# Attention: one turned unit in eight copied by ScalarE, six probability slots, and layer three's denominators inverted once a head

## The reference

```python
attn = jnp.einsum('bhqd,bhkd->bhqk', q, k)          # q, k, v quantised to 255 levels
attn = jax.nn.softmax(attn.astype(jnp.float32), axis=-1)
attn = _fq_unsigned(attn, axis=-1)                  # rounded to 0..255 of the row's maximum
out = jnp.einsum('bhqk,bhkd->bhqd', attn, v)
```

```python
kv_summary = jnp.einsum('bhsd,bhse->bhde', k, v)
k_sum = k.sum(axis=-2)
z = 1.0 / (jnp.einsum('bhld,bhd->bhl', q, k_sum)[..., None] + EPS)
attn = jnp.einsum('bhld,bhde->bhle', q, kv_summary) * z
out = attn * gate @ Wo.T
```

## Time and profile before

| what | value |
|---|---|
| median of 3 runs | 1017.53 us (1016.32 to 1019.76) |
| the profiled execution, its own time | 1022.85 us |
| its span | 1020.3 us |
| busy: TensorE, VectorE, ScalarE, GpSimd | 865.2, 736.0, 446.2, 166.8 us |
| layer two's attention loop, first row maximum to the end of the last | 579.35 to 762.64 us |
| layer three's attention | 842.82 to 898.56 us |

### The profile page before, as it was taken

One profiled execution on the slowest core, in us unless ns is written; L12 is line 12 of the kernel. 1 busy time (PEld: TensorE's weight loads), 2 busy tenths in 40 slices (PEclk: granted clock), 3 DMA queues, 4 the chain that ended last, 5 costly groups with the idle time before them and its releaser, 6 DMA issues.

```text
span 1020.3 us, 11627 instructions
## 1 busy us (share of the span) xinstructions
PE 865.2 (85%) x4214; PEld 512.5 (50%) x4214; DVE 736.0 (72%) x974; ACT 446.2 (44%) x679; POOL 166.8 (16%) x251
## 2 busy tenths in 40 slices
PE   5989894489889999989899677788888988779898
PEld 3434662244655555545455344344444657654566
DVE  1776558964557787787678898899994546658777
ACT  2214446642324422221223588789883434622111
POOL 1000000000013532425200162111111000001412
PEclk9899885589979999999899855555558999969999
DMA  8502003100132222240112989987771000000000
GB/s 266 197 3 44 1 0 50 19 2 7 19 48 43 36 35 25 54 59 10 22 25 42 170 150 176 155 146 146 139 145 30 9 1 0 1 1 1 10 11 21
DMA packets 211612, 59.13 MB, mean 58 GB/s; under 512 B 192398, under 2 KB 209892, under 8 KB 211556
## 3 DMA queue, kind: packets, MB, share of 16 engines
q1 hardware_dynamic: 211444, 58.23, 29.5%
q10 hardware_dynamic: 112, 0.17, 0.1%
HBM read 20.62 MB, written 1.05 MB: 21 GB/s over the span
## 4 chain that ended last, share of the span: by engine, by line
PE 52%; DVE 25%; ACT 10%; issue 7%; DMA 4%; POOL 1%; ACTq 1%; DVEq 0%; SPq 0%; POOLq 0%
PE ps L946 48%; ACT xc L1889 5%; DMA arena<-xc 4%; DVE arena L2593 3%; DVE arena L2227 1%; PE ps L1077 1%; DVE arena L2602 1%; PE ps L1389 1%; DVE xc L2399 1%; ACT arena_split L1806 1%; DVE sq L2506 1%; DVE sq L2503 1%; PE ps L472 1%; DVE xn_t L2028 1%; DVE arena L2141 1%
## 5 line engine op out<-in xcount | busy, mean ns | idle before, releaser
L946 PE MATMUL ps<-arena 128*128 128x16 f16 (+7 forms) x1760 | 269.1, 324 | 50.5 <-ACT xc L1889 37.5
L946 PE MATMUL ps<-arena_split 128*128 128x512 f32 (+6 forms) x736 | 199.5, 435 | 18.3 <-DVE arena_split L2405 5.7
L946 PEld LDWEIGHTS ps<-arena 128*128 128x128 f16 (+4 forms) x1760 | 132.4, 130 | 163.1 <-issue 82.5
L946 PEld LDWEIGHTS ps<-arena_split 128*128 128x128 f32 (+6 forms) x736 | 134.4, 196 | 90.3 <-issue 41.0
L1889 ACT ACTIVATE xc<-ps,arena 128x1024 int16<-128x1024 f32 x128 | 153.1, 1201 | 25.8 <-POOL arena L904 13.2
L2593 DVE TENSOR_REDUCE arena<-ps 128x1 f32<-128x1024 f32 x128 | 150.8, 1218 | 13.3 <-PE ps L946 11.0
L946 PE MATMUL ps<-sq,arena 128*64 128x256 f32 (+3 forms) x256 | 80.8, 516 | 8.1 <-DVE sq L2506 8.1
L904 POOL TENSOR_SCALAR arena<-arena 128x1 f32<-128x1 f32 x128 | 34.2, 267 | 182.4 <-DVE arena L2593 182.1
L853 POOL TENSOR_SCALAR arena<-arena 128x512 f32<-128x512 f32 x12 | 23.1, 1924 | 246.8 <-DVE arena L2421 246.8
L1658 ACT ACTIVATE act_buf<-ps 128x512 f32<-128x512 f32 (+2 forms) x34 | 20.3, 597 | 89.4 <-PE ps L946 89.3
L946 PE MATMUL ps<-mean_w,sq 128*128 128x1 f32 x240 | 35.8, 279 | 21.3 <-ACT sq L1623 21.3
(11 more groups left out here) (290 smaller groups left out, 1331.5 us busy)
## 6 DMA issues: line engine op xcount, KB each, us to landing
arena<-in_L_ffn_w SPq DMA_DIRECT2D x4, 640.0 KB, 6.0
arena_split<-arena_split SPq DMA_DIRECT2D x59, 32.0 KB
arena<-xc SPq DMA_TRANSPOSE x96, 3.3
arena<-in_x SPq DMA_DIRECT2D x1, 1024.0 KB, 5.7
arena<-in_ctx SPq DMA_DIRECT2D x1, 1024.0 KB, 8.2
arena<-in_L_xattn_Wkv SPq DMA_DIRECT2D x2, 512.0 KB, 3.9
arena<-in_L_ffn_gate_w SPq DMA_DIRECT2D x1, 1024.0 KB, 10.0
arena<-in_L_ffn_up_w SPq DMA_DIRECT2D x1, 1024.0 KB, 12.5
```

The source lines that it names most:

```text
L946: return pe.matmul(o, l, r, start=start, stop=stop)
```

## The change

In the loop: units with u mod 8 = 7 are copied out of PSUM bank 7 by ScalarE, as 512 32-bit integers a partition (two 16-bit values each), behind exponential u + 3; VectorE keeps those with u mod 8 = 3. There are six probability slots, two of them in `sq`. Exponential 4 waits once for the turned value rows, since those were read out of `sq`. Values lag seven units, so the tile's output step moves one unit too, and the query transposes are issued at other units.

In layer three: `dd` has one column for each head. The denominators come out with tokens on partitions (the queries are the stationary operand), 32 a partition; they are inverted there, widened to 16 equal columns a head (`lx_wide`), and turned back by four transposes into bank 3 (`spread`), which TensorE does between queries and gates of the next batch. VectorE then multiplies them by the gate, and that by the numerators.

```diff
+        att_more = sq[:, :, :].rearrange("p k t -> p (k t)").bitcast(I16).rearrange("p (s t) -> p s t", t=TOK)
+        PROBS = 6
...
-        dd = c3([BATCH, KC, P])
+        dd = c3([BATCH, KC, P // HD])
+        lx_inv = c3([2 * HEADS])
+        lx_wide = c3([2 * HEADS, HD])
...
-        VALUES_LAG = 6
-        QUERIES_AT = (20, 28, 36, 44)
+        VALUES_LAG = 7
+        QUERIES_AT = (8, 22, 36, 50)
...
+        def probs(u):
+
+            i = u % PROBS
+            return att_y[:, i, :] if i < 4 else att_more[:, i - 4, :]
...
+        def copied_by_act(u):
+
+            return u % 8 == 7
...
             if by_pe(u):
-                return att_copied, u // 4 + 1
+                return (att_copied_act if copied_by_act(u) else att_copied_dve), u // 8 + 1
...
+            def spread(b):
+
+                pe.wait_ge(lx_inverse, b + 1)
+                heads = P // HD
+                for m in range(KC):
+                    for j in range(2):
+                        last = pe.transpose(ps[:, 3, m * SEQ + j * P:m * SEQ + (j + 1) * P],
+                                            lx_wide[:, HEADS * j + m * heads:HEADS * j + (m + 1) * heads, :].rearrange(
+                                                "p a d -> p (a d)"),
+                                            ident[:, :])
+                last.then_inc(lx_att, 1)
...
-                for j, w in enumerate((bd, dd)):
+                for j in range(2):
                     for m in range(KC):
-                        last = mm(ps[:, 2 + j, m * SEQ:(m + 1) * SEQ], w[:, b, m, :], lx_q[:, b % 2, m, :], True, True)
+                        at = HEADS * j + m * P // HD
+                        last = mm(ps[:, 3, at:at + P // HD], lx_q[:, b % 2, m, j * P:(j + 1) * P], dd[:, b, m, :], True, True)
+                last.then_inc(lx_dens, 1)
+                for m in range(KC):
+                    last = mm(ps[:, 2, m * SEQ:(m + 1) * SEQ], bd[:, b, m, :], lx_q[:, b % 2, m, :], True, True)
                 last.then_inc(lx_att, 1)
...
-                if u >= 4:
-
-                    act.wait_ge(*probs_read(u - 4))
-                act.activation(att_y[:, u % 4, :].rearrange("p (a b) -> p a b", a=2), ps[:, score_banks(u), :], ACT.Exp,
+                if u == 4:
+                    act.wait_ge(v_turned, 16 * KC)
+                if u >= PROBS:
+
+                    act.wait_ge(*probs_read(u - PROBS))
+                act.activation(probs(u).rearrange("p (a b) -> p a b", a=2), ps[:, score_banks(u), :], ACT.Exp,
...
+            def probs_copy(u):
+
+                act.wait_ge(att_pe_turned, u // 4 + 1)
+                if u >= 8:
+
+                    act.wait_ge(att_v, u - 7)
+                act.activation(att_yt[:, u % 8].rearrange("p a b -> p (a b)").bitcast(I32), ps[:, 7, :].bitcast(I32), ACT.Copy
+                               ).then_inc(att_copied_act, 1)
...
+            for u in range(UNITS + 3):
+                if u < UNITS:
+                    exponentials(u)
+                if u >= 3 and copied_by_act(u - 3):
+                    probs_copy(u - 3)
...
-                if u >= 4 and by_pe(u - 4):
+                if u >= 4 and by_pe(u - 4) and not copied_by_act(u - 4):
                     probs_copy(u - 4)
...
-                dve.wait_ge(lx_att, b + 1)
-                step(TS(lx_den, ps[:, 3, :].rearrange("p (k t) -> p k t", k=KC), 1e-6, None, ALU.add))
-                step(dve.reciprocal(lx_den, lx_den))
+                dve.wait_ge(lx_dens, b + 1)
+                if b:
+                    dve.wait_ge(lx_att, 2 * b)
+                step(TS(lx_inv, ps[:, 3, 0:2 * HEADS], 1e-6, None, ALU.add))
+                step(dve.reciprocal(lx_inv, lx_inv))
+                dve.tensor_copy(lx_wide, b3(lx_inv, HD)).then_inc(lx_inverse, 1)
...
-                step(TTN(lx_den, ps[:, 2, :].rearrange("p (k t) -> p k t", k=KC), lx_den, ALU.mult))
                 dve.wait_ge(lx_act, 2 * b + 2)
+                dve.wait_ge(lx_att, 2 * b + 2)
+                step(TTN(lx_share, ps[:, 3, :].rearrange("p (k t) -> p k t", k=KC), lx_gate[:, b % 2], ALU.mult))
...
-                TTN(lx_o[:, b % 2], lx_den, lx_gate[:, b % 2], ALU.mult).then_inc(lx_or, 1)
+                TTN(lx_o[:, b % 2], ps[:, 2, :].rearrange("p (k t) -> p k t", k=KC), lx_share, ALU.mult).then_inc(lx_or, 1)
```

More of the change, by code:

```diff
@@ L287, in build @@
         lx_gate = c([2, KC, SEQ])
-        lx_den = c([KC, SEQ])
+        lx_share = c([KC, SEQ])
         lx_o = c([2, KC, SEQ])
@@ L319, in build @@
         exp_in, exp_out = sem("exp_in"), sem("exp_out")
-        wk_d, wk_g, wk_decay, wk_in, wk_mix, wk_den, wk_inv = (sem(n) for n in (
-            "wk_d", "wk_g", "wk_decay", "wk_in", "wk_mix", "wk_den", "wk_inv"))
+        wk_d, wk_g, wk_decay, wk_mix, wk_den, wk_inv = (sem(n) for n in (
+            "wk_d", "wk_g", "wk_decay", "wk_mix", "wk_den", "wk_inv"))
         rt_logits, rt_wd, rt_wdt, rt_wdt_sb, rt_flat, rt_gt, rt_gatest, rt_gates_sb = (sem(n) for n in (
@@ L346, in build @@
             "lx_made", "lx_copied", "lx_min_r", "lx_exp_r", "lx_keys", "lx_sum", "lx_bd"))
-        lx_qg, lx_qmin_r, lx_act, lx_qf, lx_att, lx_or, lx_x = (sem(n) for n in (
-            "lx_qg", "lx_qmin_r", "lx_act", "lx_qf", "lx_att", "lx_or", "lx_x"))
+        lx_qg, lx_qmin_r, lx_act, lx_qf, lx_dens, lx_inverse, lx_att, lx_or, lx_x = (sem(n) for n in (
+            "lx_qg", "lx_qmin_r", "lx_act", "lx_qf", "lx_dens", "lx_inverse", "lx_att", "lx_or", "lx_x"))
         xt_turned, xt_copied, xq_ready, xq_turned, xq_copied = (sem(n) for n in (
@@ L914, in _ @@
                                ALU.mult).then_inc(lx_bd, 1)
-            pool.tensor_tensor(dd.rearrange("p b m c -> p (b m) c"),
-                               head_mask[:, :].unsqueeze(1).to_broadcast([P, n, P]),
-                               lx_ks[:, :, :].rearrange("p b m -> p (b m)").unsqueeze(2).to_broadcast([P, n, P]), ALU.mult).then_inc(lx_bd, 1)
+            pool.tensor_tensor(dd.rearrange("p b m a -> p (b m) a"),
+                               head_mask[:, :].rearrange("p (a d) -> p a d", d=HD)[:, :, 0].unsqueeze(1).to_broadcast([P, n, heads]),
+                               lx_ks[:, :, :].rearrange("p b m -> p (b m)").unsqueeze(2).to_broadcast([P, n, heads]),
+                               ALU.mult).then_inc(lx_bd, 1)
             def back_scaled(v, scale, n):
@@ L1452, in batch, with query_and_gate @@
                 return slice(b * SEQ, (b + 1) * SEQ)
-            def query_and_gate(b):
+            def query_and_gate(b, between=None):
                 if b:
@@ L1463, in query_and_gate @@
                     last.then_inc(lx_qg, 1)
+                    if between and j == 0:
+                        between()
+            def spread(b):
[8 more added lines that the diff above has]
+                last.then_inc(lx_att, 1)
             pe.wait_ge(lx_bd, 3)
@@ L1478, in _ @@
                 if b + 1 < BATCH:
-                    query_and_gate(b + 1)
+                    query_and_gate(b + 1, lambda: spread(b))
+                else:
+                    spread(b)
                 if b == 2:
@@ L1885, in exponentials @@
                 act.wait_ge(att_bias, u + 1)
-                if u >= 4:
-                    act.wait_ge(*probs_read(u - 4))
-                act.activation(att_y[:, u % 4, :].rearrange("p (a b) -> p a b", a=2), ps[:, score_banks(u), :], ACT.Exp,
+                if u == 4:
[3 more added lines that the diff above has]
+                act.activation(probs(u).rearrange("p (a b) -> p a b", a=2), ps[:, score_banks(u), :], ACT.Exp,
                                bias=att_small["bias"][:, u % 3:u % 3 + 1], scale=att_small["sq"][:, t, i:i + 1],
                                accum_out=att_small["z"][:, t, i:i + 1]).then_inc(att_exp, 1)
-            for u in range(UNITS):
-                exponentials(u)
+            def probs_copy(u):
[9 more added lines that the diff above has]
+                    probs_copy(u - 3)
             act.wait_ge(att_v, UNITS)
@@ L2621, in tile_out @@
                 dve.wait_ge(att_v, (t + 1) * HEADS)
-                dve.reciprocal(A["rz"], A["z"][:, t, :]).then_inc(att_rz, 1)
-                dve.wait_ge(att_rz, t + 1)
+                step(dve.reciprocal(A["rz"], A["z"][:, t, :]))
                 STT(o_tok[:, t, :].rearrange("p (h d) -> p h d", d=HD),
```

11 lines of the change are left out of this document (5 added, 6 removed).

## The result

The changed kernel took 1017.18 us (median of 15 runs, 1014.07 to 1020.35), the kernel before 1019.81 on the same chip (15 runs): ratio 0.9962, 95% interval 0.9947 to 0.9976. By the ratio that is 3.9 us less (2.4 to 5.4), where 7.9 less was forecast; the two medians are 2.6 apart. The profiled execution has a span of 1016.7 us, the one of before 1020.3. The spans alone would mislead: the attention loop begins at 582.00 here and at 579.35 before, and between 576.2 and 581.2 in the other profiles of this study, before anything that the change touches. So I compare stages, each measured from a start of its own.

The account below looks back on a forecast made before the run. Two equally tight bounds were seen in the loop, VectorE (10.70 us per eight units) and a chain of waits through the engines (10.69). Loop -0.5 and layer three -7.4 gave -7.9: 1009.6 us from the 1017.53 median, range 996 to 1019.

Parts of the forecast that it names:

- circle: Loop: chain of waits through ScalarE, TensorE and VectorE per eight units; 10.64 plus 0.50 for ScalarE's copy gives 11.14 us.
- period: Loop: time from one tile's output step to the next, 16 units; 23.0 us forecast, 22.00 before.
- tile step: Loop: a tile's output step moves onto the chain of waits, 0.61 plus 0.13 lost; seven tiles cost 5.2 us.
- the stalls gone (about 8) pay for a slower circle: Loop: six slots end DMA stalls, offsetting 6.6 us of slower chain and 0.9 at tiles; loop -0.8.
- -2.2: Layer three, batch 0: the output projection starts at 855.4 instead of 857.57, 2.2 us earlier.
- -1.7: Layer three, batch 0: without idle ahead, the projection runs at full clock, 1.9 us instead of 3.6.
- +0.6: Layer three, batches 1 and 2: the new transposes stand on the path, 0.6 us more in each.
- -4.7: Layer three, batch 3: earlier inverse and projection at full clock end it 8.1 us after 885.75 instead of 12.8.
- Rival D: Layer three: only the clock there stays low, total -3.5, 1014 us; chance 0.13.
- A (the circle has slack): Loop: unseen slack, VectorE is the bound; 17.3 us less in the loop, 993 in all; A or halfway 0.22.
- B (transfers stay late): Loop: the nine DMA waits stay, loop +8.1; with layer three at 1.2 GHz 1023 us; chance 0.09.
- C (an integer copy of 1.20): Loop: ScalarE's integer copy costs 1.20, 10.5 us on top of the forecast, 1020 us; chance 0.09.

Follow-up runs that it names:

- e4: Changed kernel with ScalarE's copy one exponential later, behind exponential u + 4 instead of u + 3: 1014.02 us, ratio 0.9936.
- e12: e8 with the four query transposes issued at the old units 20, 28, 36 and 44: 1007.66 us, ratio 0.9844.
- e8: Changed kernel with all 32 copies on VectorE, values lagging six units and 128-column denominators: 1006.34 us, ratio 0.9869.
- e3: Changed kernel with all 32 copies on VectorE again, the rest kept: 1015.19 us, ratio 0.9945.
- e5: Changed kernel with denominators of 128 columns a chunk again instead of 8; inversion reads one column in 16: 1011.10 us, ratio 0.9909.
- e1: The change in the attention loop alone, layer three as in the kernel before: 1020.61 us, ratio 0.9997.
- e2: The change in layer three alone, the loop as in the kernel before: 1018.28 us, ratio 0.9976.
- e11: Changed kernel with values lagging six units instead of seven, ScalarE's copies kept: 1013.45 us, ratio 0.9899.
- e10: Layer three's change alone with 128-column denominators, the loop as in the kernel before: 1014.84 us, ratio 0.9926.
- e7: Changed kernel with four probability slots instead of six: 1023.37 us, ratio 1.0014.
- e9: The changed kernel without an edit, timed and profiled again: 1016.94 us, ratio 0.9935.
- e6: Changed kernel with all 32 copies on VectorE and values lagging six units instead of seven: 1011.46 us, ratio 0.9915.

## Why the loop came out as predicted and layer three did not

The measured 1017.18 lies in the range given (996 to 1019) and outside the forecast's own (1005 to 1014); the sign was right, and the gain half of the forecast. I set the forecast against a median of 3 runs, 1017.53; with the 1019.81 of 15 runs the same gain would be 1011.9.

**The loop held.** Forecast -0.8 us, measured -0.6. Its steps: circle 11.14 (measured 11.11), period 23.0 (23.03), tile step 0.74 (0.82), first copy 10.15 behind the first maximum (10.20), no exponential waiting for a DMA transfer (none), ScalarE's copy 0.49 to 0.60 (0.594 mean, 0.47 added). In two places luck helped. The circle's 11.14 was 10.64 + 0.50, and e4 shows 10.69 without the copy on it, so the copy costs 0.42 there: two small errors that cancel. And the -0.6 is set against one profile of before, whose loop took 182.7 and 181.0 elsewhere; what held is the changed loop's own length, 182.4 forecast (761.8 - 579.35) and 182.7 measured. The rule of the Trainium skill's "ScalarE: Activation LUTs" that I had set beside it, estimated at 0.52 added for this copy, would have been 0.05 too dear. The runs show piece by piece what "the stalls gone (about 8) pay for a slower circle" stated. From 183.3 two more slots lead to 175.7 (e12, -7.6), the new query places to 176.7 (e8, +1.0), the values' lag of seven to 177.8 (e3, +1.1), ScalarE's copy behind exponential 2 to 182.7 (the change, +4.9). The steps of 1 us rest on one profile each.

**Layer three is where the forecast failed.** -7.4 was forecast and -3.8 measured. In four legs, read from the start of a group of matmuls to the start of the next:

| leg | before | forecast | the change | e5, wide |
|---|---|---|---|---|
| first queries to the first projection | 14.75 | -2.2 | 13.83 (-0.9) | 12.56 (-2.2) |
| to the numerators of batch 2 | 14.44 | -1.7 + 0.6 | 13.28 (-1.2) | 13.27 (-1.2) |
| to the numerators of batch 3 | 13.74 | +0.6 | 15.88 (+2.1) | 14.20 (+0.5) |
| to the end of the last projection | 12.60 | -4.7 | 8.78 (-3.8) | 8.83 (-3.8) |
| sum | 55.53 | -7.4 | 51.77 (-3.8) | 48.86 (-6.7) |

The step that failed is the clock, and not at the place that I had watched. I took full clock at two projections because TensorE's idle 2.56 us would be gone, and both ran at full clock. For the first the reason is not shown, since e1's ran at full clock with the idle stretch still ahead: the -1.7 came true in part by luck. But I costed everything else from rows at 2.4 GHz, the four denominators at "0.92, the same as before", and asked nowhere what these matmuls do to the clock behind them. Right behind 16 matmuls of one column and the new ones of eight, TensorE's clock fell in batch 0, and again in batches 2 and 3. The first and third leg lost 1.3 and 1.5 by it; in e2, e3, e4 and e11, where the clock held in batch 2 and was low for longer in batch 3, the third leg is as forecast (14.2) and the last is 10.1. e5 takes nothing away but the narrowness, and both legs come out as forecast; e8, e10 and e12 repeat it. In the last leg 0.9 is missing in both kernels, with the clock low in or behind the numerators' group in both (3.05 for 2.02 at 877.65 in e5, 3.26 for sixteen transposes at 889.08 in the changed kernel); no profile has this leg without a low stretch, so that the clock is all of the 0.9 is not shown.

e5, the change as I had costed it, measured -9.3 us (-7.2 to -11.2), and the forecast's -7.9 lies in that interval. Of its excess over the change's -3.9, 2.9 us are seen in layer three's profile; the other 2.5 are within the intervals, and no profile shows where they lie.

Rival D had the size, 1014 and -3.5, and not the place: it kept the two old slow projections, and the trace shows three new slow stretches in their stead. A (the circle has slack) fell with the period of 23.03 and e3; B (transfers stay late) with the table of waits, which has no such row; C (an integer copy of 1.20) with 0.594.

**How sure the clock's cause is.** Two other readings were to be excluded. Idle time: the same idle stretches, 1.62 and 0.72, stand ahead of the same groups in e5, and behind the first of them the clock stayed up; e1's projection came at full clock behind 2.56 us of idle. Chance: kernels with the same layer three show falls at different places (the change, e7 and e9 in batches 0, 2 and 3; e2, e3, e4 and e11 in batch 0 and, longer, in batch 3), and e6 escaped all but the last. But in batch 0 it is seven of eight against none of four, and none of two where the denominators have 256 columns as before the change (the kernel before and e1), and three timed pairs have the same sign, which leaves little room for chance alone. In batch 2 the case is weaker: the three falls there began 0.9 us or less into the denominators, behind 1.63 us of idle, and five other kernels with narrow denominators had none.

Nor is layer three all of it: the mean granted clock over the whole kernel has a median of 0.850 in e5's timed executions and 0.840 in the change's (0.849 and 0.841 for e8 and e6, 0.841 and 0.839 for e10 and e2), and layer three's 0.97 for 0.90 makes only some 0.004 of the 0.010. Stages that no edit touches vary as well: ahead of the loop the profile of the change shows a granted clock of 0.90 over 582.0 us, e9's, of the same program, 0.92 over 580.0, and e5's 0.92 over 576.2.

The busy share of the trace doesn't tell the two apart: in the 3.81 us ahead of the fall TensorE is busy for 3.71 in the changed kernel and in e5. (The 6.90 of 7.00 in the window of the changed kernel is no cause: half of that window ran at 1.2 GHz, where the same matmuls take longer.) The Trainium skill, "TensorE: Matmul & The Clock Gate", Part 1, has the gate follow how busy the array has been. Read with the trace's busy column that rule doesn't tell the two kernels apart, and the measurement decides. The same part lets the point of a change vary from run to run; the two profiles of the changed kernel agree, with the first fall at 7.5 and at 7.2 us. What was not tried: filling up the 16 one-column matmuls, which both forms have. Alone, ahead of wide denominators, they brought no fall in batch 0; whether the eight-column ones would do it alone stays open.

## What to carry to other kernels

Before work is moved to an engine "with time to spare", close the circle that the critical item runs through all engines and ask whether the new place is on it: one place further back the same copy was free, here it cost 4.9 us. Work that is made smaller on TensorE can cost more than it saves: cost narrow matmuls together with the clock of what follows them, and read the granted clock of every stage, not only where it was low before. Where a change has several parts, price each by a kernel of its own, since here two more slots paid for the parts that lost.

## What the runs showed of the hardware that I had not expected

- A group of twelve matmul records with denominators of 8 or of 128 columns takes the same 2.02 us at full clock; but in batch 0 the rows behind the narrow ones ran at 1.2 GHz in seven profiles of eight, those behind the wide ones in none of four.
- The mean granted clock of the same stage, with the same code of the stage, was 0.91 in one program (before) and 0.94 in another (e1), and 0.90 or 0.97 with narrow denominators (the change and e6): a projection that ran at 1.2 GHz in one profile ran at 2.4 GHz in the other, so a gain that rests on the clock of one profile is uncertain. Over the whole kernel it varied from 0.837 to 0.847 in 15 executions of the changed kernel.
- ScalarE copied 128x512 32-bit integers from PSUM in 0.594 us, no dearer than the same shape in f32, and what it adds to a full queue was 0.47.
- VectorE's copy within SBUF that widens 128x32 to 128x512 took 0.43, where its products that read 128x512 from PSUM take 0.69.
